# Batch norm parameters computed inside the recurrence's block, a first z without its bias, and a first spread of v from two queues

## The chip, the cores and the metric

The kernel runs on one core of a Trainium2 chip. The metric is device time in microseconds. Before the change three runs gave 737.8, 738.04 and 739.01 us, with a median of 738.04 us.

## The reference

Two layers are computed, one after the other, on `x` and `ctx` of shape (64, 64, 256), all float32. The first is a cross attention whose output goes through a batch norm over all 64 sequences; the second is an RWKV block (token shift, five mixed projections, a recurrence with a state per head, group norm, a gated output and a feed-forward part). Cut to what matters:

```python
# layer 0: cross attention, then batch norm per channel c over batch and t
f   = softmax(phi(ctx)^T theta(x));  w_y = Wz (f g(x)) + bz           # (b, c, t)
w_y = gamma * (w_y - mean) * rsqrt(var + EPS) + beta                  # mean, var over (b, t)
x   = w_y + x
# layer 1: one RWKV block, rows are (b, c), features are t
xn  = layernorm(x) * ln1_w + ln1_b
sx  = token_shift(xn)
x5  = xn + sx * (maa_stack + tanh((xn + sx * maa_x) @ maa_w1) @ maa_w2)
w, r, k, v, g = projections of x5
for t in tokens:  out_t = r_t . (u * a + s);  s = a + w_t * s         # a = k_t v_t
x   = x + (groupnorm(out) * g) @ Wo.T
x   = x + sigmoid(xr @ Wr.T) * (relu(xk @ Wk.T) ** 2 @ Wv.T)
```

The batch norm of the kernel is z = bna * w_y + x + bnb, where bna = gamma * rstd and bnb = beta - mean * bna, both one number per partition (a partition is one channel of one of two sequences). The layer norm that follows goes over the 256 features of a row, so a number that is constant along a row, such as bnb, drops out of it; it stays in the residual.

## The kernel before

**Stages.** `program` calls three functions, and each opens a block of its own with one instruction stream for each engine; all engines meet at the end of a block. `attention` (lines 68 to 403) handles 32 pairs of sequences and leaves the unnormalised result of all of them in the buffer `wyz` with batch norm statistics in `stats`. `norm_params` (406 to 461) turns the statistics into `bna` and `bnb`. `rwkv` (464 to 1436) walks over 8 chunks of 8 sequences (512 tokens, four tiles of 128 rows).

**norm_params.** It is one chain of small operations: VectorE aggregates the statistics (443), TensorE averages the two halves of the partitions (428), VectorE forms the deviation (445 to 451), TensorE averages again (431), VectorE adds epsilon (453), GpSimd raises to the power -1/2 (439), and VectorE makes `bna` (456), a product (458) and `bnb` (460). TensorE fills its waits with blank matmuls, `warm` (line 65), 2, 2 and 6 calls of them; each call shows up as two instructions in the trace.

**rwkv.** The order of the work is written out by hand for each engine: `fill_pass(-1)` prepares chunk 0, `first_pass(0)` starts its recurrence and prepares chunk 1, and `body(n)` does in a steady state the recurrence of chunk n, the end of chunk n - 1 and the preparation of chunk n + 1. `last_pass` and `drain_pass` end it. Three parts of a chunk are named a (preparation), b (recurrence) and c (output). Engines hand work to each other through semaphores.

**The start of rwkv.** VectorE clears `eps` and a column of `ps_w` (1420, 1422). ScalarE adds `bnb` to the four tiles of x of chunk 0 (`a_bias(0)`, 1005). VectorE computes z (`a_z(0)`, 1235) and its moments (`a_zm(0)`, 1223 to 1229). GpSimd makes the reciprocal deviations (646, 648). ScalarE normalises (`a_norm(0)`, 1018), TensorE, after 17 calls of `warm`, transposes (759), and ScalarE makes `xn` out of it (`a_xn`, 1031). In `fill_pass` of ScalarE the bias of chunk 1 (`a_bias(1)`) stands ahead of `a_xn(0)`. VectorE then makes `sx` and `xm` (1243, 1246), and TensorE runs the mixes and projections in the order w0, w1, dec1, w2, v, w3, k, w4, r through three PSUM banks in turn; a bank is free again when its reader has copied it (`a_bank`). The banks go by position in `A_ORDER` modulo 3, so k0 takes the bank of v1.

**The spread of v.** SyncE waits for a half of v (`v_ready`) and issues eight DMAs for it (`spread_v`, 610 to 615); each copies all 128 rows of `v[h]`, 256 KB, into the 16 partitions i, i + 8, i + 16, ... of `vb[h]`. The queue also carries the loads of x (608) and the stores (619). The state product `b_kv(0, 0, 0)` on VectorE (1279) waits for all eight of half 0; it is the last step of VectorE's `fill_pass`. On the ScalarE side v is copied out of PSUM by `a_copy` (1059), first half 0, then half 1.

```python
for i in range(S):                                                    # spread_v, SyncE, S = 8
    sp.dma_start(vb[h][i:P:S, :, :], v[h][:, :]).then_inc(v_spread[h], 16)
```

Of the kernel before, what the change touches and what calls it, by code (L numbers as in the profile page):

```python
# [17 lines left out]
P = 128  # L18
# [387 lines left out]
def norm_params(nc, sem, t):  # L406

    s_loc, s_mean, s_dev, s_var = sem("local_moments"), sem("mean_done"), sem("deviation_ready"), sem("var_done")
    s_ve, s_pw, s_par, s_half = sem("var_eps_ready"), sem("bn_rstd_ready"), sem("bn_params_ready"), sem("pow_exponent_ready")
    ctx = ExitStack()  # L410
    with ctx:
        mv = ctx.enter_context(nc.sbuf_tensor("mv", [P, 8], F32))
        ps = ctx.enter_context(nc.psum_tensor("ps_bn", [P, 512], F32))
        ps2 = ctx.enter_context(nc.psum_tensor("ps_bn2", [P, 512], F32))
        spare = ctx.enter_context(nc.psum_tensor("ps_spare", [P, 512], F32))
        block = ctx.enter_context(nc.Block())
        half = t["cst"][:, HALF, :]

        def warm(count):
            keep_warm(nc, t["cst"][:, ID, :], t["cst"][:, 0:2, :].rearrange("p a b -> p (a b)"), spare, count)  # L420

        @block.tensor
        def _(pe):

            pe.wait_ge(t["s_late"], 16 * LATE)
            warm(WARM_A)
            pe.wait_ge(s_loc, 1)
            nc.tensor.matmul(ps[:, 0:2], half, mv[:, 0:2], start=True, stop=True).then_inc(s_mean, 1)
            warm(WARM_B)
            pe.wait_ge(s_dev, 4)  # L430
            nc.tensor.matmul(ps2[:, 0:2], half, mv[:, 4:6], start=True, stop=True).then_inc(s_var, 1)
            warm(WARM_C)

        @block.gpsimd
        def _(pool):
            nc.gpsimd.memset(t["mhalf"][:, :], -0.5).then_inc(s_half, 1)  # L436
            pool.wait_ge(s_half, 1)
            pool.wait_ge(s_ve, 1)
            nc.gpsimd.tensor_tensor(mv[:, 6:7], mv[:, 6:7], t["mhalf"][:, 0:1], ALU.pow).then_inc(s_pw, 1)

        @block.vector
        def _(dve):
            nc.vector.bn_aggr(mv[:, 0:2], t["stats"][:, :, :].rearrange("p a s -> p (a s)")).then_inc(s_loc, 1)
            dve.wait_ge(s_mean, 1)
            nc.vector.tensor_copy(mv[:, 2:3], ps[:, 0:1]).then_inc(s_dev, 1)
            dve.wait_ge(s_dev, 1)
            nc.vector.tensor_tensor(mv[:, 3:4], mv[:, 0:1], mv[:, 2:3], ALU.subtract).then_inc(s_dev, 1)
            dve.wait_ge(s_dev, 2)
            nc.vector.tensor_tensor(mv[:, 5:6], mv[:, 3:4], mv[:, 3:4], ALU.mult).then_inc(s_dev, 1)
            dve.wait_ge(s_dev, 3)  # L450
            nc.vector.tensor_tensor(mv[:, 4:5], mv[:, 1:2], mv[:, 5:6], ALU.add).then_inc(s_dev, 1)
            dve.wait_ge(s_var, 1)
            nc.vector.tensor_scalar(mv[:, 6:7], ps2[:, 0:1], EPS, None, ALU.add).then_inc(s_ve, 1)
            dve.wait_ge(s_pw, 1)
            dve.wait_ge(t["s_late"], 16 * LATE)
            nc.vector.tensor_tensor(t["bna"][:, :], mv[:, 6:7], t["bnv"][:, 0:1], ALU.mult).then_inc(s_par, 1)
            dve.wait_ge(s_par, 1)
            nc.vector.tensor_tensor(mv[:, 7:8], mv[:, 2:3], t["bna"][:, :], ALU.mult).then_inc(s_par, 1)
            dve.wait_ge(s_par, 2)
# [4 lines left out]
def rwkv(nc, sem, t, d, out):  # L464
# [60 lines left out]
    with ctx:  # L525
# [42 lines left out]
        def ab(name):  # L568
            return abank[A_ORDER.index(name) % 3]
# [972 lines left out]
```

## Time and profile before

| what | value |
|---|---|
| median of 3 runs | 738.04 us (737.8 to 739.01) |
| the profiled execution | 742.99 us |
| its span, first to last instruction | 741.2 us |
| busy: TensorE, VectorE, ScalarE, GpSimd | 643.7, 635.1, 361.4, 261.5 us |
| mean granted TensorE clock | 0.965 |

Times in rows are microseconds from the start of the span unless marked ns. A timeline row gives start, length, engine, line, operation, output and inputs, the number of instructions merged into it, and in square brackets the idle time of the engine before it and what ended that. PE is TensorE, DVE is VectorE, ACT is ScalarE, POOL is GpSimd; SPq is the queue of SyncE, which issues DMAs. A float32 matmul shows up as two instructions.

### The profile page before, as it was taken

The page shows a single profiled execution, that of the slowest core. Times are in us where ns is not written, and L with a number is a line of the kernel's source. Part 1 is how long each engine was busy: PE and PEld are TensorE (multiplying, and loading weights), DVE is VectorE, ACT ScalarE, POOL GpSimd, SP SyncE. Part 2 cuts the span into 40 slices and gives each one's busy share as a digit, 9 for nine tenths or more (in the row PEclk, how much of TensorE's full clock was granted, in tenths as well). Part 3 has the DMA queues.
Part 4 walks back from the last instruction along what each step waited for, and adds up shares of the span by engine and source line. Part 5 has one row for each costly group of instructions (what it writes and reads, how often), then busy time and mean ns, then how long its engine had stood idle before and what let it go on. Part 6 is the DMA issues. An engine that isn't in the chain of part 4 may idle for free.

```text
span 741.2 us, 9706 instructions
## 1 busy us (share of the span) xinstructions
PE 643.7 (87%) x2736; PEld 357.0 (48%) x2736; DVE 635.1 (86%) x988; ACT 361.4 (49%) x797; POOL 261.5 (35%) x187
## 2 busy tenths in 40 slices
PE   7689999988996878999899889899989988956986
PEld 5456666666542324453444435445344443523574
DVE  2499999995568999999999999999999999879623
ACT  3468888872341317446245444644625543352431
POOL 1850000001013674654536336355453633831000
PEclk9689999999999988999999999999999999987899
DMA  2611221110084146055152523705615232360000
GB/s 63 214 45 57 64 63 57 57 57 29 1 162 93 37 82 137 1 114 129 43 113 61 108 53 60 170 0 113 133 38 113 67 75 60 73 124 0 2 27 28
DMA packets 38314, 54.17 MB, mean 73 GB/s; under 512 B 4626, under 2 KB 21170, under 8 KB 38162
## 3 DMA queue, kind: packets, MB, share of 16 engines
q1 hardware_dynamic: 36866, 50.46, 30.5%
q0 software_dynamic: 1424, 3.43, 1.4%
q8 instruction: 10, 0.16, 0.1%
q14 instruction: 14, 0.11, 0.1%
HBM read 16.13 MB, written 4.19 MB: 27 GB/s over the span
## 4 chain that ended last, share of the span: by engine, by line
DVE 31%; PE 18%; issue 15%; POOL 4%; ACT 4%; DMA 2%; SPq 1%; DVEq 1%; POOLq 0%; ACTq 0%
DVE state L1292 13%; PE ps_a L765 4%; PE ps_c L851 3%; PE ps_a L794 3%; DVE x L1255 3%; DMA vb<-v 2%; POOL state L664 2%; DVE st L1223 2%; DVE state L1279 2%; PE ps_a L777 2%; PE ps_c L765 1%; DVE sx L1336 1%; POOL x L669 1%; DVE sx L1317 1%; SPq L615 1%
## 5 line engine op out<-in xcount | busy, mean ns | idle before, releaser
L669 POOL TENSOR_TENSOR x<-x,xn 128x1024 f32<-128x1024 f32 x35 | 87.5, 2501 | 198.4 <-DVE x L1255 198.4
L1292 DVE TENSOR_TENSOR_SCAN state<-ps_w,state 128x512 f32<-128x512 f32 x128 | 145.8, 1198 | 0.7
L765 PE MATMUL ps_a<-x,wsq 128*128 128x512 f32 x256 | 120.0, 609 | 5.9 <-ACT xn L1031 3.0
L664 POOL TENSOR_TENSOR state<-vb,k 128x2016 f32<-128x2016 f32 x23 | 107.2, 4661 | 24.7 <-DMA vb<-v 16.5
L1297 DVE TENSOR_TENSOR vb<-state,r 128x2048 f32<-128x2048 f32 x32 | 97.5, 3048 | 1.7
L765 PEld LDWEIGHTS ps_a<-x,wsq 128*128 128x128 f32 x256 | 48.2, 194 | 67.0 <-issue 54.8
L794 PE MATMUL ps_a<-mix_t,w 128*128 128x512 f32 x128 | 62.5, 610 | 15.6 <-DVE x L1255 9.6
L1255 DVE SCALAR_TENSOR_TENSOR x<-ps_a,vec,sx 128x512 f32<-128x512 f32 x80 | 57.3, 743 | 12.4 <-PE ps_a L794 11.1
L296 ACT ACTIVATE probs<-ps_f,negmax 128x256 f32<-128x256 f32 x128 | 59.0, 473 | 2.0 <-DVE negmax L345 1.2
L646 POOL TENSOR_TENSOR rs<-ve,mhalf 128x4 f32<-128x4 f32 x16 | 25.9, 1618 | 79.7 <-DVE ve L1229 79.7
L345 DVE TENSOR_REDUCE negmax<-ps_f 128x2 f32<-128x512 f32 x64 | 41.2, 685 | 7.4 <-PE ps_f L218 5.0
L794 PEld LDWEIGHTS ps_a<-mix_t,w 128*128 128x128 f32 x128 | 22.5, 189 | 50.4 <-DVE x L1255 17.3
L355 DVE TENSOR_SCALAR probs<-probs,rowinv 128x256 f32<-128x256 f32 x128 | 42.8, 376 | 2.2
L436 POOL MEMSET mhalf<- 128x4 f32 x1 | 0.1, 103 | 124.8 <-POOLq L92 124.8
L218 PE MATMUL ps_f<-thph 32*128 32x256 f32 x256 | 37.7, 410 | 7.1 <-ACT probs L296 7.1
L1018 ACT ACTIVATE zn<-wyz,rs 128x256 f32<-128x256 f32 (+1 forms) x64 | 33.2, 589 | 21.9 <-POOL rs L648 21.9
L765 PE MATMUL ps_c<-zn,wsq 128*128 128x512 f32 x64 | 31.9, 644 | 11.1 <-DVE zn L1321 11.1
L831 PE MATMUL ps_att<-vb,pick 128*32 128x512 f32 x256 | 33.3, 628 | 6.9 <-DVE vb L1297 6.7
L241 PE MATMUL ps_av<-probsT,gz 128*64 128x256 f32 x256 | 35.8, 400 | 3.3 <-issue 2.1
L228 PE MATMUL ps_t<-cst,probs 128*128 128x128 f32 x256 | 37.1, 289 | 1.5 <-DVE probs L355 1.4
L1088 ACT ACTIVATE wyz<-ps_c 128x512 f32 (+1 forms) x16 | 9.6, 597 | 58.7 <-PE ps_c L865 58.7
L228 PEld LDWEIGHTS ps_t<-cst,probs 128*128 128x128 f32 x256 | 28.8, 146 | 13.4 <-DVE probs L355 11.1
(168 smaller groups left out, 1248.8 us busy)
## 6 DMA issues: line engine op xcount, KB each, us to landing
vb<-v SPq DMA_DIRECT2D x128, 256.0 KB, 5.8
x<-in_x SPq DMA_DIRECT2D x32, 128.0 KB, 2.1
c<-in_ctx SPq DMA_DIRECT2D x32, 128.0 KB, 2.1
x_chunk<-in_x SPq DMA_DIRECT2D x8, 512.0 KB, 7.4
out<-sx SPq DMA_DIRECT2D x8, 512.0 KB, 3.5
wsq<-in_wsq POOLq DMA_DIRECT2D x1, 1024.0 KB, 5.3
wsq<-in_wsq POOLq DMA_DIRECT2D x1, 768.0 KB, 6.9
s<-in_s POOLq DMA_DIRECT2D x1, 512.0 KB, 7.7
```

Of the source, the lines that this page charges most:

```text
L218: mm = nc.tensor.matmul(ps_f[e][:, T * i:T * i + T], tp[r:r + CI, T + P * i:T + P * i + P], tp[r:r + CI, 0:T], start=True, stop=True)
L228: mm = nc.tensor.transpose(ps_t[e][:, T * j + P * i:T * j + P * i + P], pr[2 * p + e][:, i, P * j:P * j + P], ident)
L296: mm = nc.scalar.activation(pr[b][:, i, :], ps_f[e][:, T * i:T * i + T], ACT.Exp, bias=nm[b][:, i:i + 1], accum_out=rs[b][:, i:i + 1])
L345: nc.vector.tensor_reduce(nm[2 * p + e][:, :], ps_f[e][:, :].rearrange("p (i j) -> p i j", i=2), AX.X, ALU.max, negate=True).then_inc(s_ma ...
L355: nc.vector.tensor_scalar(pr[b][:, i, :], pr[b][:, i, :], ri[b][:, i:i + 1], None, ALU.mult).then_inc(s_scl, 1)
L664: nc.gpsimd.tensor_tensor(st[q][:, :, :, 1:L], src[:, :, :, 0:L - 1], wide(k[p][h][:, :])[:, :, :, 0:L - 1], ALU.mult).then_inc(kv_at(n, h ...
L669: nc.gpsimd.tensor_tensor(x5[j % 2][:, :, :], x5[j % 2][:, :, :], xn[:, :, 1:L1], ALU.add).then_inc(x5_ready, 1)
L765: mm = nc.tensor.matmul(bank[:, :], wsq[:, weight, c, P * o:P * o + P], src(c), start=(c == 0), stop=(c == EC - 1))
L794: nc.tensor.matmul(bank[:, :], lhs, rhs, start=True, stop=True).then_inc(a_done, 1)
L1255: nc.vector.scalar_tensor_tensor(x5[j % 2][:, NB * c:NB * c + NB, :], bt(ab(name)[:, :]), col(STK0 + MIX_OF[j], c), sx[:, NB * c:NB * c + ...
L1292: nc.vector.tensor_tensor_scan(row, w[h][:, :], row, 0.0, ALU.mult, ALU.add).then_inc(scanned, 1)
L1297: nc.vector.tensor_tensor(src, st[q][:, :, :, :], wide(r[p][h][:, :]), ALU.mult).then_inc(prod_ready, 1)
```

## The change

The block of `norm_params` goes away. Its instructions move into the streams of `rwkv`, behind the clearing of `eps` and `ps_w` on VectorE; the 6 last calls of `warm` are dropped. The two averages go to banks of `ps_a`. The first z is computed as bna * w_y + x, right after `bna`; the product and `bnb` follow later; ScalarE adds `bnb` to the four finished tiles of `wyz` in `first_bias`, behind `a_tanh(0)`. `a_bias(0)` is gone, and in ScalarE's `fill_pass` `a_xn(0)` now stands ahead of `a_bias(1)`. Of the eight DMAs of the first spread (chunk 0, half 0) SyncE issues i = 0 to 3, and ScalarE issues i = 4 to 7 between its copies of v0 and v1.

```diff
-def norm_params(nc, sem, t):
...
-        @block.tensor
-            pe.wait_ge(t["s_late"], 16 * LATE)
-            warm(WARM_A)
-            pe.wait_ge(s_loc, 1)
-            nc.tensor.matmul(ps[:, 0:2], half, mv[:, 0:2], start=True, stop=True).then_inc(s_mean, 1)
-            warm(WARM_B)
-            pe.wait_ge(s_dev, 4)
-            nc.tensor.matmul(ps2[:, 0:2], half, mv[:, 4:6], start=True, stop=True).then_inc(s_var, 1)
-            warm(WARM_C)
...
@@ spread_v @@
-                for i in range(S):
+                for i in range(S // 2 if h == 0 and isinstance(n, int) and n == 0 else S):
                     sp.dma_start(vb[h][i:P:S, :, :], v[h][:, :]).then_inc(v_spread[h], 16)
@@ gpsimd, ahead of rstd(0) @@
+            nc.gpsimd.memset(t["mhalf"][:, :], -0.5).then_inc(s_half, 1)
+            pool.wait_ge(s_half, 1)
+            pool.wait_ge(s_ve, 1)
+            nc.gpsimd.tensor_tensor(mv[:, 6:7], mv[:, 6:7], t["mhalf"][:, 0:1], ALU.pow).then_inc(s_pw, 1)
@@ tensor @@
+            half = cst[:, HALF, :]
+            pe.wait_ge(t["s_late"], 16 * LATE)
+            warm(WARM_A)
+            pe.wait_ge(s_loc, 1)
+            nc.tensor.matmul(abank[0][:, 0:2], half, mv[:, 0:2], start=True, stop=True).then_inc(s_mean, 1)
+            warm(WARM_B)
+            pe.wait_ge(s_dev, 4)
+            nc.tensor.matmul(abank[1][:, 0:2], half, mv[:, 4:6], start=True, stop=True).then_inc(s_var, 1)
             warm(WARM_D)
             fill_pass(-1)
@@ scalar @@
+            def first_bias():
+                act.wait_ge(zn_ready, TILES)
+                nc.scalar.activation(wyz[:, 0:TILES, :], wyz[:, 0:TILES, :], ACT.Identity, bias=t["bnb"][:, 0:1]).then_inc(z0_biased, 1)
@@ a_copy @@
                     nc.scalar.activation(dst[h][:, :], ab(f"{letter}{h}")[:, :], ACT.Copy).then_inc(sem_out, 1)
+                    if letter == "v" and h == 0 and isinstance(n, int) and n == 0:
+                        act.wait_ge(v_ready, 1)
+                        for i in range(S // 2, S):
+                            act.dma_start(vb[h][i:P:S, :, :], v[h][:, :]).then_inc(v_spread[h], 16)
@@ scalar fill_pass @@
+                a_xn(n + 1)
                 a_bias(n + 2)
-                a_xn(n + 1)
                 state_column(n + 1, 0, 0)
                 a_tanh(n + 1)
+                first_bias()
                 a_dec(n + 1)
@@ scalar, start @@
-            a_bias(0)
             a_norm(0)
+            act.wait_ge(s_par, 3)
             fill_pass(-1, 1)
@@ a_z @@
-                dve.wait_ge(x_biased, n + 1)
+                dve.wait_ge(x_biased, n)
@@ vector, start @@
             dve.wait_ge(init_done, 3)
-            a_z(0)
+            nc.vector.bn_aggr(mv[:, 0:2], t["stats"][:, :, :].rearrange("p a s -> p (a s)")).then_inc(s_loc, 1)
+            dve.wait_ge(s_mean, 1)
+            nc.vector.tensor_copy(mv[:, 2:3], abank[0][:, 0:1]).then_inc(s_dev, 1)
...
+            dve.wait_ge(s_var, 1)
+            nc.vector.tensor_scalar(mv[:, 6:7], abank[1][:, 0:1], EPS, None, ALU.add).then_inc(s_ve, 1)
+            dve.wait_ge(s_pw, 1)
+            dve.wait_ge(t["s_late"], 16 * LATE)
+            nc.vector.tensor_tensor(t["bna"][:, :], mv[:, 6:7], t["bnv"][:, 0:1], ALU.mult).then_inc(s_par, 1)
+            dve.wait_ge(s_par, 1)
+            dve.wait_ge(x_in, 16)
+            first = wyz[:, 0:TILES, :]
+            nc.vector.scalar_tensor_tensor(first, first, t["bna"][:, 0:1], xr_in[:, :, :], ALU.mult, ALU.add).then_inc(z_ready, 1)
+            nc.vector.tensor_tensor(mv[:, 7:8], mv[:, 2:3], t["bna"][:, :], ALU.mult).then_inc(s_par, 1)
             a_zm(0)
+            dve.wait_ge(s_par, 2)
+            nc.vector.tensor_tensor(t["bnb"][:, :], t["bnv"][:, 1:2], mv[:, 7:8], ALU.subtract).then_inc(s_par, 1)
             fill_pass(-1, 1)
@@ program @@
-        norm_params(nc, sem, t)
```

## Rows read from the trace of the kernel before

**Rows 1.** The page: busy time of VectorE, and the granted clock in 40 slices.

```profile
DVE 2499999995568999999999999999999999879623
...
PEclk9689999999999988999999999999999999987899
```

**Rows 2.** The timeline of all engines, 173 to 181 us: norm_params and the first z.

```profile
173.11 1.02 DVE L443 BATCH_NORM_AGGREGATE mv<-stats 128x2 f32<-128x192 f32 x1 [0.53 <-PEq L92]
...
175.65 2.84 PE L65 MATMUL ps_spare<-cst 128*128 128x256 f32 x12
...
176.13 0.59 POOL L439 TENSOR_TENSOR mv<-mv,mhalf 128x1 f32<-128x1 f32 x1 [2.96 <-DVE mv L453]
176.75 0.16 DVE L456 TENSOR_TENSOR bna<-mv,bnv 128x1 f32<-128x1 f32 x1 [0.77 <-POOL mv L439]
...
177.14 0.16 DVE L460 TENSOR_TENSOR bnb<-bnv,mv 128x1 f32<-128x1 f32 x1
...
178.78 7.58 PE L65 MATMUL ps_att<-cst 128*128 128x256 f32 x34 [0.30 <-PEq L411]
178.81 0.06 DVE L1420 MEMSET eps<- 128x1 f32 x1 [1.51 <-PEq L411]
...
179.00 1.15 ACT L1005 ACTIVATE x_chunk<-x_chunk,bnb 128x1024 f32<-128x1024 f32 x1 [6.88 <-DVE ps_w L1422]
180.27 1.28 DVE L1235 SCALAR_TENSOR_TENSOR wyz<-wyz,bna,x_chunk 128x1024 f32<-128x1024 f32 x1 [1.32 <-ACT x_chunk L1005]
```

**Rows 3.** The same view, 185 to 189 us: ScalarE ahead of the first xn.

```profile
185.09 2.07 ACT L1018 ACTIVATE zn<-wyz,rs 128x256 f32<-128x256 f32 x4 [4.94 <-POOL rs L648]
187.07 1.14 ACT L1005 ACTIVATE x_chunk<-x_chunk,bnb 128x1024 f32<-128x1024 f32 x1
...
188.11 1.42 ACT L1031 ACTIVATE xn<-ps_a,vec 128x512 f32<-128x512 f32 x2
```

**Rows 4.** The same view near the end of the span: the same step in drain_pass.

```profile
718.18 2.07 ACT L1018 ACTIVATE zn<-wyz,rs 128x256 f32<-128x256 f32 x4 [3.53 <-POOL rs L648]
...
721.00 1.45 ACT L1094 ACTIVATE xn<-ps_c,vec 128x512 f32<-128x512 f32 x2 [0.75 <-PE ps_c L759]
```

**Rows 5.** The timeline of ScalarE, 192 to 209 us: its waits in fill_pass.

```profile
194.32 0.60 ACT L1036 ACTIVATE mix_t<-ps_a 128x512 f32<-128x512 f32 x1 [4.63 <-PE ps_a L777]
201.88 0.60 ACT L1041 ACTIVATE low_t<-ps_a 128x512 f32<-128x512 f32 x1 [6.96 <-PE ps_a L805]
...
206.34 0.60 ACT L1059 ACTIVATE v<-ps_a 128x512 f32<-128x512 f32 x1 [3.72 <-PE ps_a L765]
208.06 0.60 ACT L1059 ACTIVATE v<-ps_a 128x512 f32<-128x512 f32 x1 [1.12 <-PE ps_a L765]
```

**Rows 6.** The issues of the spread of v: one window, then all 128 of the run.

```profile
206.97 10.98 SPq L615 DMA_DIRECT2D vb<-v  x16
...
L615 SPq DMA_DIRECT2D vb<-v x128: 532/644/1216, 207.0 to 652.9; - x128
```

**Rows 7.** The chain of waits: from the last issue to the landing.

```profile
211.82 7.41 DMA vb<-v
```

**Rows 8.** The timeline of VectorE, 214 to 222 us: the end of fill_pass.

```profile
214.14 1.54 DVE L1255 SCALAR_TENSOR_TENSOR x<-ps_a,vec,sx 128x512 f32<-128x512 f32 x2 [0.34 <-PE ps_a L794]
215.72 1.23 DVE L1259 TENSOR_TENSOR x<-x,xn 128x1024 f32<-128x1024 f32 x1
219.26 2.26 DVE L1279 TENSOR_TENSOR state<-vb,k 128x2016 f32<-128x2016 f32 x1 [2.32 <-DMA vb<-v]
```

**Rows 9.** DMA traffic, 205 to 235 us, in 40 slices of 0.75 us.

```profile
DMA  0000699999999999999999999999999995000000
GB/s 0 0 0 0 120 328 227 213 188 210 186 251 210 188 210 186 205 191 251 205 191 210 189 205 191 251 205 191 205 188 194 203 337 161 0 0 0 0 0 0
```

**Rows 10.** The timeline of TensorE: the projections of k (chunk 0) and v (chunk 1).

```profile
209.58 3.60 PE L765 MATMUL ps_a<-x,wsq 128*128 128x512 f32 x8
...
248.91 5.40 PE L765 MATMUL ps_a<-x,wsq 128*128 128x512 f32 x8 [2.94 <-POOL x L669]
```

**Rows 11.** Busy time by stretch: start:end, length, PE, PEld, DVE, ACT, POOL, then clock.

```profile
249.40:252.80 3.40, 3.40 (x5) 1.35 (x4) 3.40 (x4) 0.49 (x1) 2.57 (x1) 0.50 0.00 0
```

More of the change, by code:

```diff
@@ L403, in _ @@
             dve.wait_ge(s_bn, PAIRS)
-def norm_params(nc, sem, t):
[L408 to L420, printed above, removed]
-        @block.tensor
-        def _(pe):
-            pe.wait_ge(t["s_late"], 16 * LATE)
-            warm(WARM_A)
-            pe.wait_ge(s_loc, 1)
-            nc.tensor.matmul(ps[:, 0:2], half, mv[:, 0:2], start=True, stop=True).then_inc(s_mean, 1)
-            warm(WARM_B)
-            pe.wait_ge(s_dev, 4)
-            nc.tensor.matmul(ps2[:, 0:2], half, mv[:, 4:6], start=True, stop=True).then_inc(s_var, 1)
-            warm(WARM_C)
[L434 to L459, printed above, removed]
-            nc.vector.tensor_tensor(t["bnb"][:, :], t["bnv"][:, 1:2], mv[:, 7:8], ALU.subtract).then_inc(s_par, 1)
-            dve.wait_ge(s_par, 3)
@@ L493, in rwkv @@
     c_done = sem("c_matmuls_done")
+    z0_biased = sem("first_z_biased")
+    s_loc, s_mean, s_dev, s_var = sem("local_moments"), sem("mean_done"), sem("deviation_ready"), sem("var_done")
+    s_ve, s_pw, s_par, s_half = sem("var_eps_ready"), sem("bn_rstd_ready"), sem("bn_params_ready"), sem("pow_exponent_ready")
     init_done = sem("init_done")
@@ L557, in rwkv @@
         kk = sb("kk", [P, EC, TOK])
+        mv = sb("mv", [P, 8])
         abank = [pb(f"ps_a{i}") for i in range(3)]
@@ L1425, in _ @@
             dve.wait_ge(init_done, 3)
-            a_z(0)
+            nc.vector.bn_aggr(mv[:, 0:2], t["stats"][:, :, :].rearrange("p a s -> p (a s)")).then_inc(s_loc, 1)
+            dve.wait_ge(s_mean, 1)
+            nc.vector.tensor_copy(mv[:, 2:3], abank[0][:, 0:1]).then_inc(s_dev, 1)
+            dve.wait_ge(s_dev, 1)
+            nc.vector.tensor_tensor(mv[:, 3:4], mv[:, 0:1], mv[:, 2:3], ALU.subtract).then_inc(s_dev, 1)
+            dve.wait_ge(s_dev, 2)
+            nc.vector.tensor_tensor(mv[:, 5:6], mv[:, 3:4], mv[:, 3:4], ALU.mult).then_inc(s_dev, 1)
+            dve.wait_ge(s_dev, 3)
+            nc.vector.tensor_tensor(mv[:, 4:5], mv[:, 1:2], mv[:, 5:6], ALU.add).then_inc(s_dev, 1)
+            dve.wait_ge(s_var, 1)
[8 more added lines that the diff above has]
+            nc.vector.tensor_tensor(mv[:, 7:8], mv[:, 2:3], t["bna"][:, :], ALU.mult).then_inc(s_par, 1)
             a_zm(0)
+            dve.wait_ge(s_par, 2)
+            nc.vector.tensor_tensor(t["bnb"][:, :], t["bnv"][:, 1:2], mv[:, 7:8], ALU.subtract).then_inc(s_par, 1)
             fill_pass(-1, 1)
```

## The prediction

> **What bounds the kernel now.** I read the page first. VectorE is busy at nine tenths or more from slice 13 to slice 34 [rows 1], so the steady state is VectorE's, and nothing in the change touches it. The two gaps are at the ends: VectorE shows 5, 5, 6, 8 in slices 9 to 12 (167 to 222 us), and that is where the change works. There the engines wait for each other one by one, so I read the timeline of all engines from the end of attention and asked at each step which wait ends last. Then came the chain of waits for the spread of v, the DMA traffic, and the granted clock.
>
> The start is one chain [rows 2]: aggregate at 173.11, power on GpSimd until 176.72, bna at 176.75, bnb at 177.14. Then nothing is computed until 178.81: TensorE works off twelve blank matmuls from 175.65 to 178.49, and the block cannot end before they do. Then come the clearing of eps, ScalarE's bias (1.15 us) and at 180.27 z. Between bna and z lie 3.52 us.
>
> The end of the fill is the second place [rows 8]: VectorE has nothing left to do at 216.95 and starts the state product at 219.26, when the eight DMAs of half 0 have landed, 7.41 us after the last of them was issued [rows 7]. All that follows hangs on this product. First passes and bodies are relative chains, so a shift of the product should reach the end of the span whole.
>
> **The parts.**
>
> *The block boundary, the blank matmuls and a_bias(0).* In the new order z follows bna as one small VectorE instruction follows another: bna to bnb are two steps in 0.39 us, so 0.20 us a step [rows 2]. That takes out 3.52 - 0.20 = 3.32 us. Against it, the clearing of eps and ps_w, at present beside nothing, now stands ahead of the aggregate: from its start at 178.81 to the first instruction that waits for it at 179.00, 0.19 us [rows 2]. The product mv[7] now stands between z and its moments; it costs between 0 and its 0.16 us (the length of bna's own row), and I take 0.10, since it can overlap with the tail of z. The first part is 3.32 - 0.19 - 0.10 = 3.03 us.
>
> bnb itself moves behind the moments. It is needed when ScalarE leaves a_norm(0), 2.07 us of work that starts only after GpSimd's power, while bnb is ready within half a microsecond of the moments: cost nothing, its cover is a_norm.
>
> *TensorE's blank matmuls.* The 34 that remain take 7.58 us [rows 2]. They now start when the second average is done, about 176.0 in the new time, and end at 183.6. The normalised tiles are ready at 187.16 [rows 3] less 3.03, 184.13. So they don't hold up the transposes, by 0.5 us. Were that margin gone, each call more would cost 0.45 us. The gap ahead of the transposes is no longer than today's (186.36 to 187.2), so I expect the clock to stay.
>
> *xn ahead of the bias of chunk 1.* Today ScalarE ends zn at 187.16, runs the bias of chunk 1, and begins xn at 188.11 [rows 3]: 0.95 us behind zn. With ScalarE free the same step in drain_pass begins 721.00 - 720.25 = 0.75 us behind it [rows 4], since it waits for the transposes. That is 0.20 us. The bias (1.14 us) slides into the wait of 4.63 us ahead of the tanh [rows 5]. Its data are a load on SyncE's queue that moves forward with z, so it isn't late either.
>
> *first_bias.* 1024 elements a partition, as a_bias: 1.14 us behind the tanh, where ScalarE idles for 6.96 us until 201.88 [rows 5]. Nothing. The next reader of these tiles is the output projection in body(1). Without that cover it would delay low_t and everything behind by 1.14 us.
>
> *The spread from two queues.* Three terms. First the issues. SyncE takes 10.98 us for sixteen with the wait for v1 in them, and 532 to 1216 ns for one, median 644 [rows 6]. No row shows ScalarE issuing a DMA. The bounds are therefore 0.53 and 1.22 us each; I take SyncE's 0.64, because it is the same transfer. Four take 2.56 us, from 206.97 to 209.53. The second copy of v, now at 208.06 [rows 5], is queued behind them: it runs from 209.55 to 210.15. Who waits for it is TensorE: k0 takes the bank of v1, and k started at 209.58 with no gap [rows 10]. It now starts at 210.17, 0.6 us later. The mix w4 behind it and VectorE's instructions on it, which waited for TensorE (0.34 us [rows 8]), go with it, so VectorE is done at 217.55 rather than 216.95. The copies of k, the norm of chunk 1 and r on ScalarE have idle time ahead of them and absorb it. SyncE's issues for half 1 start later too (210.2), which nobody feels: its queue was still issuing half 0 until 212.5, and the load of x behind them is due only some 30 us later.
>
> Second the transfers. All DMA engines are busy from 208.75 us on, at about 200 GB/s [rows 9]; eight transfers of 256 KB at that rate are 10.5 us, from 208.3 to 218.8, which is the landing that we see. The issues (0.64 us) run ahead of the transfers (1.3 us each), so quicker issues alone change nothing. But 200 GB/s is not all that these engines can do: the second slice shows 328, and the plateau is broken by 251 in slices 12, 19 and 26, seven slices or 5.25 us apart [rows 9]. That is four transfers, the place where i goes from 3 to 4 or from 7 to the next 0. So transfers 0 to 3 hinder each other in a way in which 3 and 4 don't. In the new order SyncE's queue holds 0 to 3 and ScalarE's 4 to 7, and both kinds are in flight at once. I expect a rate between those two rows, 251 GB/s: 2.1 MB in 8.4 us, landed at 216.7, before VectorE is free. At the low end, 200 GB/s, nothing is gained; at 328 it lands at 214.7, which brings no more than 216.7 does.
>
> The Trainium skill, "SBUF — State Buffer", section "Door 1: The DMA port swizzle", says that bits 2 to 4 and bit 6 of the partition number pick one of 16 ports; by it transfers 0 to 3 reach one set of eight ports and 4 to 7 the other eight. The peaks four transfers apart agree with that. The skill's "DMA: Bandwidth & Descriptors", section "Issuing engines are not separate DMA queues", speaks against this part: issuing from a second engine only saves sequencer time. By the first the spread gets faster, by the second this term is zero; it is a rival below.
>
> Third, the product starts at 217.58 instead of 219.26: 1.68 us. What is late next is VectorE itself, through TensorE's w4.
>
> **Sum.** 3.03 + 0.20 + 0 + 1.68 = 4.91 us. Against the profiled execution (span 741.2, in all 742.99) that is 736.3 and 738.1. That execution stands 4.95 us above the median of the runs; I assume the shift is the same in both: 738.04 - 4.91 = 733.1 us.
>
> **The clock.** The projection of v of chunk 1 takes 5.40 us at 248.91 against 3.60 for the same eight at full clock [rows 10], since the granted clock is 0.50, the level of 1.2 GHz, from 249.4 to 252.8 [rows 11], after TensorE had idled 2.94 us. This stands on the chain. The idle time stays, but it comes 5 us earlier, and where the clock falls may move: 1.8 us either way.
>
> **The rivals.**
>
> *The second queue brings nothing.* The transfers share the same engines, the last one lands when it does now. The 200 GB/s plateau with every engine at nine tenths [rows 9] speaks for it, the peaks against. Issues at the upper end (1.22 us) belong here too: v1 then waits until 211.85, k starts at 212.47, 2.9 us late, and the product starts at 219.9, 0.6 us later than now. Time: 738.04 - 3.23 = 734.8, or 735.4 with the slow issues. Chance 0.28.
>
> *The fall of the clock at 249 goes away or becomes shorter*: 4.91 + 1.8, 731.3 us. For it: shorter waits on TensorE earlier in the fill. Against it: the wait of 2.94 us ahead of it is unchanged. Chance 0.08.
>
> *Slower: ScalarE's queue stalls on its issues.* Place: between the copies of v0 and v1. If ScalarE could not issue while the DMA engines have a backlog, each issue would last as long as a transfer or two. Price: every microsecond beyond 209.58 - 0.60 delays k, w4 and the product by one. The product gains nothing once an issue takes 1.07 us (4 x 1.07 = 4.3, a delay of 2.3 us). To eat the 3.23 us as well takes 1.88 us an issue, to be slower by 0.2% (1.5 us, about the least that a measurement of this kernel can tell from no change) 2.25 us. At 2.5 us it would be 738.04 + 2.5 = 740.5 us. Against it: the longest of 128 issues is 1.216 us [rows 6]. Chance 0.05.
>
> *No change within 0.2%.* Not one mechanism but the issues between 1.5 and 2.2 us, or the slow issues together with a longer stretch at the lower clock: 735.4 + 1.8 = 737.2. Chance 0.07.
>
> **How the numbers follow.** The forecast, 733.1, has 0.52. With the rival without a faster spread and the one with the better clock, faster by over 0.2% has 0.88; same 0.07; slower 0.05. The range starts at 730.7 (the better clock, and 0.6 for issues that cost nothing) and ends at 736.0 (slow issues 735.4, and 0.6 for small terms of the front). Outside it I leave the last two cases and a little of the others.
>
> **What would show it.** In the profile after, z should start about 0.2 us behind bna and near 177.2, and xn about 0.75 us behind zn. The first spread should show above 230 GB/s while both queues are at work, and the product of VectorE should follow its last add without a wait for a DMA, near 214.3 (217.58 less 3.23). ScalarE should show four issues of about 0.64 us. If a wait for the DMA of some 2 us stands ahead of the product, the rival without a faster spread is right. If v1 is copied over 4 us behind v0, the issues are dear. If the total gain differs from the shift of the product, the clock or the steady state took or gave the rest.

## The result, and the profile after

The changed kernel takes 738.2 us (median of 20 runs, 730.73 to 745.52), the kernel before 741.42 us in 20 runs of the same comparison (737.5 to 745.36). The ratio is 0.9941, with a 95% interval from 0.9917 to 0.9966. That is 0.59% or 4.4 us faster (2.5 to 6.2). The ratio leaves out the four longest runs of the changed kernel (742.03 us and more) as slow ones, and none of the kernel before; with all runs kept, the medians are only 3.2 us apart. The change was forecast at 4.91 us, which the interval of the ratio holds. The absolute time doesn't: 738.2 lies above the range of 730.7 to 736.0. And, as the intervals below show, the parts that make up the change are not all those that I forecast.

The profiled execution of the changed kernel took 737.07 us, its span is 735.3 us against 741.2. The page, busy time of VectorE and granted clock:

```profile
DVE  2699999984577999999999999999999999879623
...
PEclk9899999999999979999999999999999999987999
```

The steady state is as before [rows 1]. The clock is different in the first slices, before anything that the change touches; I come back to that. The timeline of the start (all engines), which answers to rows 2 and 3:

```profile
168.29 0.06 DVE L1387 MEMSET eps<- 128x1 f32 x1 [0.56 <-PEq L92]
...
168.53 1.02 DVE L1393 BATCH_NORM_AGGREGATE mv<-stats 128x2 f32<-128x192 f32 x1
...
170.56 0.16 DVE L1395 COPY mv<-ps_a 128x1 f32<-128x1 f32 x1 [1.00 <-PE ps_a L944]
...
173.19 0.16 DVE L1406 TENSOR_TENSOR bna<-mv,bnv 128x1 f32<-128x1 f32 x1 [0.77 <-POOL mv L666]
173.38 1.28 DVE L1410 SCALAR_TENSOR_TENSOR wyz<-wyz,bna,x_chunk 128x1024 f32<-128x1024 f32 x1
174.58 0.15 DVE L1411 TENSOR_TENSOR mv<-mv,bna 128x1 f32<-128x1 f32 x1
...
178.27 2.07 ACT L976 ACTIVATE zn<-wyz,rs 128x256 f32<-128x256 f32 x4 [11.01 <-POOL rs L594]
...
181.15 1.45 ACT L993 ACTIVATE xn<-ps_a,vec 128x512 f32<-128x512 f32 x2 [0.81 <-PE ps_a L709]
```

z follows bna after 0.19 us, where it was 3.52 [rows 2]. xn follows zn after 0.81 us, where it was 0.95 [rows 3]. The wait of 1.00 us for the first average is new: it was 0.47 us before. The end of the fill on ScalarE, VectorE and TensorE, which answers to rows 5, 8 and 10:

```profile
199.40 0.60 ACT L1021 ACTIVATE v<-ps_a 128x512 f32<-128x512 f32 x1 [3.72 <-PE ps_a L715]
200.03 4.35 ACTq L1025 DMA_DIRECT2D vb<-v  x4
204.72 0.60 ACT L1021 ACTIVATE v<-ps_a 128x512 f32<-128x512 f32 x1 [4.73 <-issue]
...
211.80 1.54 DVE L1222 SCALAR_TENSOR_TENSOR x<-ps_a,vec,sx 128x512 f32<-128x512 f32 x2 [4.95 <-PE ps_a L744]
213.37 1.23 DVE L1226 TENSOR_TENSOR x<-x,xn 128x1024 f32<-128x1024 f32 x1
214.52 2.25 DVE L1246 TENSOR_TENSOR state<-vb,k 128x2016 f32<-128x2016 f32 x1
...
205.47 5.37 PE L715 MATMUL ps_a<-x,wsq 128*128 128x512 f32 x8 [2.67 <-ACT v L1021]
```

Here is the first surprise. The product no longer waits for a DMA: the spread has indeed become faster. But ScalarE's four issues last 4.35 us and not 2.56, v1 is copied 4.7 us behind v0, TensorE waits 2.67 us for its bank, and the projection of k then takes 5.37 us rather than 3.60. The busy time by stretch shows the clock of the two stretches at half, at the averages and at k (start:end, length, PE, PEld, DVE, ACT, POOL, then clock, DMA share, GB/s):

```profile
168.20:171.60 3.40, 3.35 (x9) 2.84 (x10) 1.79 (x8) 0.00 (x0) 0.10 (x1) 0.50 0.00 0
205.70:209.10 3.40, 3.40 (x5) 1.36 (x5) 1.08 (x8) 0.89 (x3) 1.21 (x2) 0.51 1.07 263
```

The DMA traffic, 197 to 227 us in slices of 0.75 us, answers to rows 9:

```profile
GB/s 11 0 0 0 0 60 208 352 232 240 330 284 262 257 259 262 229 240 197 213 188 205 194 229 219 194 213 186 208 182 223 333 104 0 0 0 0 0 0 0
```

From 202.25 us on, while both kinds of transfer are in flight, the rate is 229 to 352 GB/s; with SyncE's half 1 alone it falls back to about 200. The last transfer of half 0 lands at 210.9 us, 10.9 us behind the copy of v0 and well ahead of the product at 214.52.

**Intervals instead of spans.** Spans of single executions differ by several microseconds for one and the same kernel, so I cut every profile at the same four instructions: VectorE's first one behind attention, the first z, the end of the copy of v0, and the first product `b_kv(0, 0, 0)`. Between these points the profiles repeat to some hundredths of a microsecond, as long as the clock doesn't fall. All in us, from one profile each; the experiments are told below:

| kernel | attention | to z | to v0 | to product | to the end | all behind attention |
|---|---|---|---|---|---|---|
| before | 173.11 | 7.16 | 26.67 | 12.32 | 521.94 | 568.09 |
| changed | 168.29 | 5.09 | 26.62 | 14.52 | 520.78 | 567.01 |
| changed, again (r1) | 172.71 | 4.08 | 26.63 | 12.64 | 521.04 | 564.39 |
| SyncE issues all (e1) | 166.88 | 4.08 | 26.63 | 12.37 | 521.64 | 564.72 |
| split alone (e2) | 167.05 | 7.16 | 26.69 | 14.27 | 520.83 | 568.95 |
| issues behind v1 (e3) | 167.34 | 4.08 | 26.62 | 13.78 | 523.48 | 567.96 |
| other order, SyncE (e4) | 172.77 | 4.09 | 26.64 | 11.19 | 522.11 | 564.03 |
| other order in all (e5) | 167.73 | 4.08 | 26.64 | 11.19 | 522.26 | 564.17 |
| GpSimd issues (g1) | 167.47 | 4.09 | 26.62 | 11.80 | 522.32 | 564.83 |
| blanks ahead of k (g3) | 164.71 | 4.08 | 26.62 | 12.94 | 521.05 | 564.69 |
| ScalarE issues alone (h2) | 172.28 | 4.08 | 26.63 | 12.99 | 520.72 | 564.42 |
| xn first (f1) | 172.33 | 7.16 | 26.52 | 12.38 | 521.51 | 567.57 |
| no end blanks (f2) | 167.37 | 6.20 | 27.11 | 13.30 | 521.92 | 568.53 |
| bias kept (f3) | 172.72 | 5.70 | 26.50 | 12.33 | 522.55 | 567.08 |

### The profile page after: what moved, and what is told of

Same layout as the page of the kernel before. It is cut to its first block, busy times and chain, and to the rows that moved or that the text cites. A ratio compares the mean times of both kernels' runs of the same rounds, so it can differ in the third digit from the quotient of the medians.

```text
span 735.3 us, 9671 instructions
## 1 busy us (share of the span) xinstructions
PE 639.9 (87%) x2724; PEld 353.6 (48%) x2724; DVE 633.8 (86%) x988; ACT 361.1 (49%) x797; POOL 261.7 (36%) x187
## 4 chain that ended last, share of the span: by engine, by line
DVE 30%; PE 16%; issue 15%; POOL 4%; ACT 3%; DMA 1%; DVEq 1%; SPq 1%; POOLq 0%; ACTq 0%
DVE state L1259 13%; PE ps_a L715 4%; PE ps_c L801 3%; DVE x L1222 3%; PE ps_a L744 2%; POOL state L610 2%; DVE st L1190 2%; PE ps_c L715 2%; DVE sx L1303 1%; DVE state L1246 1%; POOL x L615 1%; PE ps_a L727 1%; DVE sx L1284 1%; PE ps_att L781 1%; DMA vb<-v 1%
## 5 line engine op out<-in xcount | busy, mean ns | idle before, releaser
L228 PE MATMUL ps_t<-cst,probs 128*128 128x128 f32 x256 | 35.6, 281 | 1.9 <-DVE probs L355 1.9
L218 PEld LDWEIGHTS ps_f<-thph 32*128 32x128 f32 x256 | 24.2, 187 | 21.2 <-issue 18.5
```

Of the source, the lines that this page charges most:

```text
L218: mm = nc.tensor.matmul(ps_f[e][:, T * i:T * i + T], tp[r:r + CI, T + P * i:T + P * i + P], tp[r:r + CI, 0:T], start=True, stop=True)
```

## The experiments

Theory A: the new start brings its 3 us; the two port sets make the spread faster; but ScalarE's issues are dear and stand ahead of its copy of v1, which costs more than the spread gains. Rivals: B, the split pays and its long interval was a chance fall of the clock; C, the faster spread comes from the second queue and not from the order of the transfers.

**e1_sync_only.** SyncE issues all eight again.

```diff
-                for i in range(S // 2 if h == 0 and isinstance(n, int) and n == 0 else S):
+                for i in range(S):
@@ a_copy @@
-                        for i in range(S // 2, S):
-                            act.dma_start(vb[h][i:P:S, :, :], v[h][:, :]).then_inc(v_spread[h], 16)
```

> The changed kernel with all eight DMAs of the first spread issued by SyncE again; the start of the recurrence stays as changed. Theory A (ScalarE's issues are dear and stand ahead of the copy of v1): from the end of the copy of v0 to the start of the product there are about 12.3 us as before the change (after it 14.5), with a wait for the DMA of about 2.3 us ahead of the product, TensorE's projection of k follows w3 without a gap, and the kernel is 2 us faster than the changed one. Theory B (the two queues do pay, and the long interval in the one profile was a chance fall of the clock): this kernel is 1 to 2 us slower than the changed one.

The timeline of VectorE and of SyncE's queue:

```profile
209.96 2.26 DVE L1242 TENSOR_TENSOR state<-vb,k 128x2016 f32<-128x2016 f32 x1 [2.38 <-DMA vb<-v]
...
197.61 10.84 SPq L561 DMA_DIRECT2D vb<-v  x16
```

The interval to the product is 12.37 us with a wait for the DMA of 2.38 us, as theory A has it, and as before the change. The ratio to the kernel before is 0.9931 (0.9894 to 0.9969), 735.13 us in 8 runs. Against the changed kernel's 0.9941 that is no difference that the whole times can show. The interval is 2.15 us shorter than in the first profile of the changed kernel, 0.27 us shorter than in the second.

**r1_changed_again.** The changed kernel, unaltered, once more.

> The changed kernel itself once more, to see which parts repeat. ScalarE's four issues should take 4.3 us again and v1 should be copied 4.7 us behind v0. The fall of the clock during k returns if the wait of TensorE brings it (interval 14.5 us) and is gone if it was chance (12.7 us). From the first instruction behind attention to z: 4.1 us if the clock holds there, 5.1 us if it falls again.

```profile
203.45 4.17 ACTq L1025 DMA_DIRECT2D vb<-v  x4
207.96 0.60 ACT L1021 ACTIVATE v<-ps_a 128x512 f32<-128x512 f32 x1 [4.55 <-issue]
...
208.70 3.67 PE L715 MATMUL ps_a<-x,wsq 128*128 128x512 f32 x8 [2.49 <-ACT v L1021]
...
216.06 2.25 DVE L1246 TENSOR_TENSOR state<-vb,k 128x2016 f32<-128x2016 f32 x1
```

These are the timelines of ScalarE, TensorE and VectorE. The issues and TensorE's wait repeat (4.17 and 2.49 us), and half 0 lands 10.6 us behind the copy of v0. The two falls of the clock don't: the start takes 4.08 us and k takes 3.67. So, from one profile each, the split costs 12.64 - 12.37 = 0.27 us by itself, and 1.7 us more when the clock falls in k. Theory A holds for the first amount, theory B is half right about the second.

**e2_split_only.** The kernel before with the split of the first spread, nothing else.

```diff
-                for i in range(S):
+                for i in range(S // 2 if h == 0 and isinstance(n, int) and n == 0 else S):
@@ a_copy @@
+                    if letter == "v" and h == 0 and isinstance(n, int) and n == 0:
+                        act.wait_ge(v_ready, 1)
+                        for i in range(S // 2, S):
+                            act.dma_start(vb[h][i:P:S, :, :], v[h][:, :]).then_inc(v_spread[h], 16)
```

> The kernel before the change with only the spread split over SyncE and ScalarE. If the split is what loses, the interval from the copy of v0 to the product is 12.7 us (clock holds) to 14.5 us (clock falls), against 12.3 us before; the start up to the copy of v0 is as before (7.16 us from attention to z, 26.67 us from there). If the loss came from the split together with the new start, it is 12.3 us or less.

```profile
206.14 5.35 PE L765 MATMUL ps_a<-x,wsq 128*128 128x512 f32 x8 [2.44 <-ACT v L1059]
```

The interval is 14.27 us, 1.95 more than before, and TensorE's timeline shows k at 5.35 us behind the same gap. The split alone loses. With the first profile of the changed kernel and r1 there are three profiles with a gap of about 2.5 us ahead of k; in two of them the clock fell.

**g3_blank_before_k.** The changed kernel with blanks in the gap.

```diff
                 a_mod(n + 1, 3)
+                warm(7)
                 a_proj(n + 1, 2, "k", WK)
```

> The changed kernel with 7 calls of blank matmuls (3.1 us) on TensorE ahead of the projection of k, where it waited 2.67 us for the copy of v1. If the fall of the clock during k comes from this wait, k takes 3.6 us here and not 5.37, and the interval from the copy of v0 to the product is 12.9 to 13.3 us (14.5 less 1.77, plus up to 0.5 for blanks that run over). If the fall has nothing to do with the wait, it can be there in spite of the blanks, 14.5 us.

k takes 3.60 us, and the interval is 12.94 us: the 14.52 less 1.77, plus 0.2 of overrun (k starts 5.66 us behind v0 instead of 5.47). In the ten profiles in which TensorE doesn't wait ahead of k, it takes 3.60 us each time. That fits a fall that comes from the gap in some executions; two falls are too few to give a rate.

**h2_scalar_alone.** SyncE waits for v1 before it issues its half of the first spread.

```diff
-                sp.wait_ge(v_ready, n * 2 + h + 1)
+                sp.wait_ge(v_ready, n * 2 + h + (2 if h == 0 and isinstance(n, int) and n == 0 else 1))
```

> The changed kernel, but SyncE waits for v1 before it issues its four of half 0, so that ScalarE issues its own four with no other engine issuing. If the 1.1 us come from two engines issuing at once, ScalarE's four take 2.6 us here (0.64 each) and v1 is copied 2.7 us behind v0. If ScalarE is slow by itself, they take 4.3 us again.

```profile
203.01 2.60 ACTq L1025 DMA_DIRECT2D vb<-v  x4
...
206.58 8.19 SPq L561 DMA_DIRECT2D vb<-v  x12
```

These rows of ScalarE's and SyncE's queues show that ScalarE is not slow by itself. Alone, it takes 2.60 us for four, 0.65 each, which is what I had assumed from SyncE's rows. SyncE's twelve take 8.19 us, 0.68 each. Where both queues are at work ScalarE takes 1.04 to 1.11 us each on average (4.17 to 4.42 for four, in five profiles). The four are not alike, as the row of the single issues shows (shortest, median and longest in ns), first of r1, then of h2:

```profile
L1025 ACTq DMA_DIRECT2D vb<-v x4: 641/826/1777, 203.4 to 205.8; - x4
```

```profile
L1025 ACTq DMA_DIRECT2D vb<-v x4: 602/628/640, 203.0 to 205.0; - x4
```

The first issue is as quick as in h2; the last one takes 1.78 us. SyncE's four of half 0 take 0.59 to 1.59 us each in r1. SyncE's twelve together last 11.79 us in r1, but that is no price of the issues alone: between the fourth and the fifth SyncE waits from 207.4 to 208.6 for v1, which ScalarE copies late. The product still starts no earlier (12.99 us), because SyncE's four transfers now come last, and it waits 1.85 us for them.

**g1_gpsimd_issues.** GpSimd issues transfers 4 to 7.

```diff
@@ gpsimd fill_pass @@
                 prev(n + 1, sx_ready, xprev, t["prev1"], xn)
+                pool.wait_ge(v_ready, 1)
+                for i in range(S // 2, S):
+                    pool.dma_start(vb[0][i:P:S, :, :], v[0][:, :]).then_inc(v_by_pool, 16)
@@ vector b_kv @@
+                if isinstance(n, int) and n == 0 and h == 0:
+                    dve.wait_ge(v_by_pool, 16 * (S // 2))
+                    dve.wait_ge(v_spread[0], 16 * (S // 2))
+                    dve.sem_inc(v_spread[0], 16 * (S // 2))
```

> The changed kernel with transfers 4 to 7 issued by GpSimd, which is idle at this time, instead of ScalarE (with a semaphore of their own that VectorE waits for and adds on). If what costs is that the issues stand ahead of ScalarE's copy of v1, this keeps the faster landing without the price: no gap of TensorE ahead of k, landing about 10.5 us behind the copy of v0, interval 10.1 to 11 us, 1.3 to 2.2 us less than with SyncE alone (12.37). If issuing from two engines at once is slow in itself (each issue 1.1 us), the last transfer starts later and the interval is 11.2 to 12 us. If the landing is no faster than from one queue, 12.3 us.

```profile
198.47 2.25 POOL L623 DMA_DIRECT2D vb<-v  x4 [21.86 <-ACT v L1025]
...
198.20 11.53 SPq L562 DMA_DIRECT2D vb<-v  x12
```

GpSimd pays only 0.56 us an issue, ScalarE and TensorE are not held up (k 3.60 us, no gap), and yet the interval is 11.80 us and not 10.1 to 11: SyncE's twelve take 11.53 us, 0.96 each, here without a wait for v1, and the last transfer of half 0 to land is SyncE's own fourth, at 209.8. In size that is the case of "issuing from two engines at once is slow in itself", but not in its cause. GpSimd's last issue ends at 200.7, and SyncE's slowest issues come behind it. So do two dear ones in e3 (told next), where ScalarE's last issue ends at 204.0. The rows of these issues, g1 and then e3:

```profile
L562 SPq DMA_DIRECT2D vb<-v x2: 1440/1670/1899, 202.1 to 204.0; - x2
```

```profile
L561 SPq DMA_DIRECT2D vb<-v x2: 1289/1317/1345, 204.9 to 206.2; - x2
```

So it isn't the moment of issuing together that makes an issue dear. At these times transfers of both queues were still on their way. But that alone isn't enough either: in h2 SyncE's first four took 0.59 to 0.62 us each while ScalarE's last transfer was still on its way (landed at 210.25). What makes the issues of two queues dear stays open. Ratio to before 0.9948 (0.9914 to 0.9981), 736.24 us in 12 runs.

**e3_issue_behind_v1.** ScalarE copies v1 first.

```diff
-                    if letter == "v" and h == 0 and isinstance(n, int) and n == 0:
-                        act.wait_ge(v_ready, 1)
+                if letter == "v" and isinstance(n, int) and n == 0:
+                    act.wait_ge(v_ready, 2)
                     for i in range(S // 2, S):
```

> The changed kernel with ScalarE's four issues moved behind its copy of v1, so that TensorE gets the bank for k at once. Theory A: no gap of TensorE ahead of k; the issues (about 1.1 us each) now delay the copy of k0 by 1 to 1.5 us; half 0 lands later than in the changed kernel but earlier than from one queue; the interval from the end of the copy of v0 to the product is 11.0 to 11.6 us. Theory B: no better than the changed kernel, 14 us.

```profile
199.79 4.25 ACTq L1025 DMA_DIRECT2D vb<-v  x4
...
211.82 2.26 DVE L1246 TENSOR_TENSOR state<-vb,k 128x2016 f32<-128x2016 f32 x1 [2.74 <-DMA vb<-v]
```

Both theories missed. TensorE's gap is gone (k 3.60 us), but the interval is 13.78 us and ends with a wait for the DMA of 2.74 us. The four issues again take 4.25 us beside SyncE's, and they start 1.7 us later than in the changed kernel. The trace also shows SyncE's transfers of half 1 landing among those of half 0: the first two, issued at 200.7 and 201.5, land at 207.8 and 210.3, and ScalarE's last one of half 0 only at 211.8. How much of the late landing comes from that, and how much from the dear issues, no run separates. Ratio to before 0.9951 (0.9922 to 0.9981).

**e4_order_one_queue and e5_order_all.** One queue, another order: in the first spread, and in all.

```diff
+                for i in (0, 4, 1, 5, 2, 6, 3, 7) if h == 0 and isinstance(n, int) and n == 0 else range(S):   # e4
+                for i in (0, 4, 1, 5, 2, 6, 3, 7):                                                             # e5
```

> All eight issues of the first spread from SyncE, in the order 0, 4, 1, 5, 2, 6, 3, 7. Theory A (transfers 0 to 3 share one set of ports, 4 to 7 the other, and what makes them fast is to have both in flight): the rate of half 0 rises from 200 to 240 GB/s or more although one queue is used, half 0 lands 1.5 to 2.3 us earlier than with the order 0 to 7, and the interval from the copy of v0 to the product is 10.0 to 10.8 us. Theory C (it is the second queue that lets the engines overlap transfers): the rate stays at 200 GB/s and the interval at 12.3 us.

> As the run before, with the new order in all sixteen spreads. Theory A: in addition GpSimd's waits for a DMA at chunk 1 (3.5 us) and chunk 7 (9.1 us) get shorter by about 2 us each; the first of them is on the chain, so 1 to 3 us faster than the run before. Theory C: the same time as with all eight issued by SyncE in the old order.

e4's DMA traffic from 197 us in slices of 0.75 us, and its product:

```profile
GB/s 0 0 0 22 11 0 0 0 0 0 117 306 273 240 224 235 240 224 238 240 221 238 240 221 199 202 197 197 194 243 210 191 208 188 205 182 265 333 21 0
...
214.69 2.26 DVE L1242 TENSOR_TENSOR state<-vb,k 128x2016 f32<-128x2016 f32 x1 [1.20 <-DMA vb<-v]
```

From one queue, in alternating order, the rate is 221 to 240 GB/s and falls back to about 200 where half 1 goes in the old order. Nothing else differs from e1. So theory C is out as the only cause, and the order of the transfers is one: the interval is 11.19 us, 1.18 less than e1's. This is less than the 1.5 to 2.3 that theory A expected. That the reason lies in the port sets is argued: it is the pattern that the order was made for, but no run tried an order that alternates without changing the set. In e5 GpSimd's wait at chunk 1 is 3.34 us where e4 has 4.48, and at chunk 7 7.89 where it has 9.24, so there too the order gives 1.1 to 1.4 us; but from the product to the end it takes 522.26 us against 522.11. The gain of 1 to 3 us that I expected didn't reach the end. On VectorE e5 is 0.95 us ahead of e4 at 54.9 us behind the product, and only 0.25 us ahead at 69.6: the difference went into the gate projection of chunk 1, 5.23 us against 4.53. About 0.2 us are left at 446 us behind the product, so the shorter wait at chunk 7 moved nothing there, and at 454 us, near the end, they are lost too. Ratios to before: e4 0.9941 (0.9916 to 0.9965), e5 0.9937 (0.9913 to 0.9962).

**f1_swap_only, f2_no_end_blanks, f3_bias_kept.** The parts of the new start.

```diff
@@ f1: kernel before, ScalarE fill_pass @@
+                a_xn(n + 1)
                 a_bias(n + 2)
-                a_xn(n + 1)
@@ f2: kernel before, norm_params @@
-            warm(WARM_C)
@@ f3: e1 with bnb ahead of z, ScalarE's bias of x ahead of z, and no first_bias @@
+            act.wait_ge(s_par, 3)
+            a_bias(0)
             a_norm(0)
-            act.wait_ge(s_par, 3)
```

> The kernel before with xn ahead of the bias of chunk 1, nothing else. xn starts 0.75 to 0.81 us behind zn and not 0.95: 0.15 to 0.2 us less from z to the copy of v0 (26.47 to 26.52 against 26.67) if the gain is passed on; 26.67 if something else on the way takes it.

> The kernel before without the six calls of blank matmuls at the end of its middle block. If they alone hold up the end of the block, it ends when bnb is done and from attention to z there are 7.16 - 1.3 = 5.8 to 6.0 us. If leaving a block costs about as much by itself, it is 6.5 us or more.

> The changed kernel with SyncE issuing all of the spread, and with the old order of z: bnb first, then ScalarE's bias of x, then z; no first_bias. The merged block alone. The bias (1.15 us) and bnb (0.4 us) and a handover each way come back: from attention to z 4.08 + 1.7 = 5.8 us, so that of the 3.08 us gained 1.4 belong to the block and its blanks and 1.7 to the z without bias. If the bias had been hidden, it is 4.1 to 4.5 us.

VectorE's timeline, f2 first, then f3:

```profile
171.01 0.16 DVE L455 TENSOR_TENSOR bna<-mv,bnv 128x1 f32<-128x1 f32 x1 [0.77 <-POOL mv L438]
...
171.40 0.16 DVE L459 TENSOR_TENSOR bnb<-bnv,mv 128x1 f32<-128x1 f32 x1
172.11 0.06 DVE L1419 MEMSET eps<- 128x1 f32 x1 [0.55 <-PEq L411]
...
173.57 1.28 DVE L1234 SCALAR_TENSOR_TENSOR wyz<-wyz,bna,x_chunk 128x1024 f32<-128x1024 f32 x1 [1.32 <-ACT x_chunk L1004]
```

```profile
176.60 0.16 DVE L1402 TENSOR_TENSOR bna<-mv,bnv 128x1 f32<-128x1 f32 x1 [0.77 <-POOL mv L666]
...
178.42 1.28 DVE L1198 SCALAR_TENSOR_TENSOR wyz<-wyz,bna,x_chunk 128x1024 f32<-128x1024 f32 x1 [1.27 <-ACT x_chunk L963]
```

f1: 26.52 us from z to v0 instead of 26.67, the 0.15 us at the lower end of what was expected, passed on whole. f2: from bna to z 2.56 us instead of 3.52. The blanks were worth 0.96 us and not 1.3, because leaving the block still takes 0.55 us (the wait ahead of L1419) when nobody is late; with the blanks it was 1.51 [rows 2]. f3: 5.70 us from attention to z, as expected. Of the 3.08 us of the new start 7.16 - 5.70 = 1.46 us belong to the merged block (the blanks among them) and 5.70 - 4.08 = 1.62 us to the z without bias. f2's later intervals (27.11 and 13.30 us) are longer than before; the clock fell from 172.5 to 175.9 us there, which fits the first; the later landing stays open.

## Why the prediction was wrong where it was

**The level.** The step that failed is the last one of the sum: "I assume the shift is the same in both: 738.04 - 4.91 = 733.1 us". The three runs shown were low for this kernel. In the comparison of 20 it takes 741.42 us, 3.4 us more, and that alone puts the changed kernel outside the range; 741.42 less 4.91 would have been 736.5. The table shows where such differences can come from. Attention, the same code in all fourteen profiles, takes between 164.71 and 173.11 us. Its length goes with the clock in the first 60 us: 172.28 to 173.11 us in the six profiles with 17 us at half clock there, 164.71 to 168.29 us in the eight with 3.4 to 10.2. Whether the low clock makes attention longer, or both come from a late start of some other part, no run tests. The busy time by stretch, 27 to 44 us, of the kernel before and then of g3, the longest and the shortest:

```profile
27.00:44.00 17.00, 12.12 (x63) 8.03 (x64) 7.03 (x16) 5.74 (x16) 14.42 (x32) 0.60 0.39 113
```

```profile
27.00:44.00 17.00, 14.97 (x108) 9.53 (x106) 13.66 (x32) 12.01 (x38) 14.18 (x32) 0.93 0.43 125
```

At a mean clock of 0.60 VectorE does 16 instructions in this stretch, at 0.93 it does 32. So 4.82 of the 5.9 us between the two spans of the profiled executions are attention's and have nothing to do with the change. The row that would have warned me is in the page: the clock in slices 2 and 3 is 6 and 8 [rows 1]. The profiled execution, 742.99 us, was a second sign. A range for an absolute time has to hold this spread; I took it from three runs that happened to lie within 1.2 us.

**The start: right.** Forecast 3.32 - 0.19 - 0.10 = 3.03 us. Measured 7.16 - 4.08 = 3.08, less 0.07 for the product behind z (6.89 us from z to the end of zn before, 6.96 after): 3.01. TensorE's 34 blanks did end ahead of zn, and first_bias was hidden. What I hadn't counted on is a fall of the clock during the two averages; in the first profile of the changed kernel it cost 1.01 us, in r1 and the seven other kernels with this start none. My sign "the product near 214.3" came out at 214.52 in that profile by luck alone, since attention happened to be 4.82 us shorter; counted from the copy of v0 the product came later than before.

**xn ahead of the bias: right**, 0.15 us (f1) for a forecast of 0.20.

**The spread: wrong, sign and size.** The term "the product starts at 217.58 instead of 219.26: 1.68 us" came out at -0.32 us (12.32 to 12.64) with the clock up and at -2.20 with the clock down. Its pieces:

- "I take SyncE's 0.64, because it is the same transfer" is the step that failed. ScalarE alone does take 0.65 (h2). But with SyncE's queue at work beside it, it takes 1.04 to 1.11 us each. The bounds (0.53 to 1.22) held this, the choice didn't. With 1.07 my own formula puts the gain at zero, close to the -0.32 measured. Most of the rest is a pause that I had at 0.02 us: ScalarE begins the copy of v1 0.34 us behind the end of its last issue (207.62 to 207.96 in r1). The rival "the second queue brings nothing" (0.28), with its slow issues, had about the right price.
- The faster landing was right in kind. The product has no wait for the DMA left in the changed kernel, and e4 shows that the order brings a part of it by itself. The size was too large: by my 216.7 half 0 would have landed 9.8 us behind the copy of v0; it took 10.9 us (10.6 in r1), against 12.4 from one queue (e1) and 11.2 from one queue in alternating order (e4). The Trainium skill's "SBUF — State Buffer", "Door 1: The DMA port swizzle", gives the bits of the partition number that pick a port; that an order alternating between the two port sets should be faster is what I worked out from it, and e4's trace agrees (221 to 240 against about 200 GB/s). By its "DMA: Bandwidth & Descriptors", "Issuing engines are not separate DMA queues", a second engine saves only issue time. The runs show that it saves little of that here: the eight issues of half 0 take 5.4 us from SyncE alone (e1) and 4.35 us shared by two engines in the changed kernel, where I had counted on half. And the landing is earlier than the rule lets expect.
- "TensorE starts k 0.6 us later" was 2.8 us (2.6 in r1), counted from the copy of v0, with a gap of 2.5 to 2.7 us where I had foreseen a short one: by my sum TensorE would have waited half a microsecond, and I named no fall of the clock for it.

**The rest of the fill, unforeseen.** In all five profiles in which v1 is held back behind ScalarE's issues (changed, r1, e2, g3, h2) the projection of v of chunk 1 takes 3.70 us, and from the product to the end there are 520.72 to 521.05 us. In seven of the other nine it takes 5.40 us (3.70 in e1 and f1), and in all nine there are 521.51 to 523.48. Between the kernel before and r1 0.8 of the 0.9 us of this difference arise in the first 69 us behind the product. In the first 45 us behind it the clock is at half for 3.4 us in four of the five profiles (6.8 in h2) and for 6.8 or 10.2 us in the nine; in e1 and f1 this is one stretch, which begins 9 us behind the product. So the fall at 249 did go away, as in my rival with the better clock (0.08), but that brought about 1 us and not 1.8. Why a later k spares a fall I didn't test.

**Together.** Behind attention the changed kernel gains 568.09 - 564.39 = 3.70 us when the clock holds (3.08 start, 0.04 up to v0, -0.32 spread, 0.90 rest) and 1.08 us when it falls twice; the measured ratio says 2.5 to 6.2. That the ratio's 4.4 stands so near the forecast 4.91 is partly luck: a miss of 2 us in one term met 1 us from another, and the profiles add up to 3.70 at best. Without the split (e1) it is 3.37 us with one term fewer to go wrong, and with the other order (e4) 4.06, the best of the fourteen. In whole times e1, e4, e5 and the changed kernel can't be told apart: their intervals overlap almost wholly.

**A slip of reading.** VectorE's 5, 5, 6, 8 stand in slices 10 to 13 of rows 1 (167 to 241 us), not in 9 to 12. Nothing hangs on it.

## What to carry to other kernels

Price an issue of a DMA by which other queue is at work at that time, and look at what stands behind it on its engine: four issues ahead of a 0.6 us copy held up a PSUM bank and through it TensorE. Before a second queue, try the order of the transfers on the one that is there; an alternating order shortened the interval by 1.2 us for nothing, though whole times couldn't show it. And when single executions of a kernel differ by more than the change is worth, cut the profiles at fixed instructions and compare intervals; take the absolute level from as many runs as can be had, or widen the range by their spread.

## What the runs showed of the hardware that I had not expected

- With a second queue at work, issues of DMAs become dear: 0.65 us for ScalarE alone, 1.04 to 1.11 on average beside SyncE; SyncE 0.68 alone, 0.96 beside GpSimd (g1). GpSimd beside SyncE took 0.56. Single issues took up to 1.9 us, some of them behind the other engine's last issue; the cause is open.
- The same transfers in another order, from one queue: 221 to 240 GB/s rather than about 200 (e4, e1).
- A gap of 2.4 to 2.7 us on TensorE was followed by a fall of the granted clock in two of three profiles (changed, e2; not r1), and then cost 1.7 us more than the gap itself.
- Leaving a block with all engines on time takes 0.55 us (f2).
- The same attention code took 164.71 to 173.11 us, and was longest in the six profiles in which the clock stayed at half for 17 us of the first 60.
